# Feed-forward: three inner layers kept with the features on the partitions, and their sum of squares as one plain product with ones

## The reference

```python
amp = jax.nn.sigmoid(x @ amp_w + amp_b)
ph = jnp.tanh(x @ ph_w + ph_b) * math.pi
h = (jnp.cos(ph) + jnp.sin(ph)) * amp
for l in range(L):                                  # L = 2
    e = h @ ent_w[l] + ent_b[l]
    ent = e @ ent_pw[l] + ent_pb[l]
    h = _layer_norm(h + ent, ln3_g[l], ln3_b[l])
    t = jnp.einsum('bsd,pdf->pbsf', h, path_w[l]) + path_b[l][:, None, None, :]
    mod = jnp.cos(phase[l]) + jnp.sin(phase[l])
    interf = jnp.sum(t * mod[:, None, None, :], axis=0)
    h = _layer_norm(h + interf, ln4_g[l], ln4_b[l])
x = _layernorm(x + h)
```

## Time and profile before

| | |
|---|---|
| median of 3 runs | 908.15 us (905.5 to 908.82) |
| the profiled execution | 906.72 us, its span 904.8 us |
| mean granted TensorE clock | 0.989 |
| PE (matmul) | 861.6 us, 95% of the span |
| PE weight load | 717.6 us, 79% |
| DVE (VectorE) | 677.2 us, 75% |
| ACT (ScalarE) | 548.4 us, 61% |
| POOL (GpSimd) | 487.0 us, 54% |
| share of PE in the chain that ended last | 59% |

### The profile page before, as it was taken

One profiled execution on the slowest core, in us unless ns is written; L12 is line 12 of the kernel. 1 busy time (PEld: TensorE's weight loads), 2 busy tenths in 40 slices (PEclk: granted clock), 3 DMA queues, 4 the chain that ended last, 5 costly groups with the idle time before them and its releaser, 6 DMA issues.

```text
span 904.8 us, 19451 instructions
## 1 busy us (share of the span) xinstructions
PE 861.6 (95%) x5812; PEld 717.6 (79%) x5812; DVE 677.2 (75%) x2060; ACT 548.4 (61%) x1666; POOL 487.0 (54%) x796
## 2 busy tenths in 40 slices
PE   6899999999899999999999999998999999999993
PEld 6778888888787888888888887776778778878773
DVE  5778888888878878777787866758884675666556
ACT  6756556666666757575656655755736645664563
POOL 3465655465856646454655521337751781593387
PEclk9999999999999999999999999999999999999997
DMA  6655353543584846575584548434002002001001
GB/s 204 228 167 174 118 166 124 174 162 129 179 265 141 255 129 211 158 233 153 160 236 137 179 125 272 169 109 148 1 24 71 0 12 82 1 1 47 1 0 47
DMA packets 79475, 117.49 MB, mean 130 GB/s; under 512 B 8480, under 2 KB 42272, under 8 KB 78752
## 3 DMA queue, kind: packets, MB, share of 16 engines
q1 hardware_dynamic: 75792, 112.81, 40.1%
q10 hardware_dynamic: 3600, 3.68, 1.3%
HBM read 58.25 MB, written 17.31 MB: 84 GB/s over the span
## 4 chain that ended last, share of the span: by engine, by line
PE 59%; DVE 6%; POOL 2%; SPq 2%; issue 2%; ACT 2%; DMA 1%; POOLq 0%; DVEq 0%; ACTq 0%
PE bank L161 45%; PE bank L1513 4%; PE bank L2040 3%; PE bank L1536 2%; PE bank L1499 2%; PE bank L1540 1%; SPq L702 1%; DVE stats L1942 1%; DVE w_ffn L1727 1%; ACT prob L1106 1%; POOL hT L1835 1%; DMA xres<-in_x 1%; PE bank L1449 1%; DVE y L1956 1%; DVE bank L1257 0%
## 5 line engine op out<-in xcount | busy, mean ns | idle before, releaser
L1106 ACT ACTIVATE prob<-bank,nmax 128x128 f32<-128x128 f32 (+1 forms) x512 | 209.6, 432 | 25.8 <-DVE nmax L1257 23.3
L161 PE MATMUL bank<-w_ffn,hT 128*128 128x512 f32 x768 | 188.5, 396 | 1.1 <-DVE w_ffn L1727 0.9
L1257 DVE CUSTOM_DVE_ANT_0 bank<-bank,mask 128x128 f32<-128x128 f32 (+1 forms) x512 | 168.2, 386 | 3.4 <-DVE cv L1202 2.3
L161 PEld LDWEIGHTS bank<-w_ffn,hT 128*128 128x128 f32 x768 | 140.2, 188 | 29.9 <-POOL hT L1835 1.4
L919 POOL TENSOR_TENSOR zone<-raw,zone 128x256 fp32r<-128x256 f32 x128 | 96.3, 785 | 59.8 <-ACT zone L1053 59.8
L1513 PE MATMUL bank<-ident,prob 128*128 128x128 f32 x768 | 119.4, 278 | 0.8 <-ACT probT L1119 0.4
L1119 ACT ACTIVATE probT<-bank 128x512 f32<-128x512 f32 x97 | 58.5, 604 | 96.3 <-PE bank L1540 96.1
L1106 ACT ACTIVATION_READ_ACCUMULATOR prob<-bank,nmax 128x1 f32 x512 | 110.9, 217 | 0.0
L161 PE MATMUL bank<-xT,w_q 128*128 128x256 f32 x768 | 102.5, 286 | 3.0 <-DVE o L1278 3.0
L161 PEld LDWEIGHTS bank<-xT,w_q 128*128 128x128 f32 x768 | 98.9, 193 | 8.0 <-issue 3.1
L1896 ACT ACTIVATE ht<-bank,cols 128x128 f32<-128x128 f32 x192 | 72.4, 459 | 53.2 <-PE bank L2040 53.2
(11 more groups left out here) (133 smaller groups left out, 1510.4 us busy)
## 6 DMA issues: line engine op xcount, KB each, us to landing
q<-stage SPq DMA_DIRECT2D x192, 128.0 KB, 2.8
k<-kstage SPq DMA_DIRECT2D x48, 256.0 KB, 4.0
x<-xres SPq DMA_DIRECT2D x16, 512.0 KB, 4.6
raw<-in_ent_wT SPq DMA_DIRECT2D x32, 256.0 KB, 4.1
raw<-in_ent_pw SPq DMA_DIRECT2D x32, 256.0 KB, 4.4
raw<-in_path_w SPq DMA_DIRECT2D x8, 512.0 KB, 3.9
xres<-in_x SPq DMA_DIRECT2D x8, 512.0 KB, 4.0
x1b<-x SPq DMA_DIRECT2D x8, 512.0 KB, 5.1
```

The source lines that it names most:

```text
L161: ins = t.matmul(out, lhs(a, k), rhs(b, k), start=first and n == 0 and m == 0, stop=last and n == len(kts) - 1 and m == 2, skip_group_chec ...
L1106: ins = s.activation(prob[:, u, c * width:(c + 1) * width], banks[u][:, c * width:(c + 1) * width], ACT.Exp, scale=-1.0, bias=nmax[:, i % ...
L1257: ins = v.tensor_tensor_reduce(scored, scored, mask[:, S - width:S], scale=-1.0, scalar=3e38, op0=ALU.add, op1=ALU.min, accum_out=nmax[:, ...
```

## The change

**Layers 0 to 2** are made turned, so that nothing is transposed back: weights are stationary, hT moves, and the four banks `z0` to `z3` of a layer hold 128 features x 512 tokens each. The mean over the features is taken out beforehand: the matrix of each layer is centred over its output features and multiplied by the gain of the layer before (`means` on ScalarE, `centre` on VectorE), and its constants go into a column `c` (`column_sum`, `column_total`, `column_centred`, `bias_partials`), of which each inner layer has one. Left is the sum of squares: ScalarE squares the four banks, GpSimd and VectorE add them up, and TensorE multiplies by ones in a single plain fp32 product (`sum_of_squares`), which puts the sum over all features on every partition. ScalarE takes the inverse root, one Newton step refines it (`inverse_of`), and the factor is applied when the next layer's banks are read (`turned_out`).

**Layer 3** is as before with tokens on the partitions; its input's factor comes from four one-column products (`second_moments`) and a power on GpSimd.

```diff
+_SCALAR = ("hi0", "sq0", "sq1", "sq2", "sq3", "hi1", "hi2", "hi3", "root", "square")
+_VECTOR = ("z0", "z1", "z2", "z3", "lo0", "pair", "total", "lo1", "lo2", "lo3", "newton", "inverse")
...
+                def turned_out(s_, j):
...
+                    if s_ == 0:
+                        ins = v.tensor_copy(y[:, j, :], bank)
+                    else:
+                        ins = v.scalar_tensor_tensor(y[:, j, :], bank, -0.5 / D, inverse[:, :], ALU.mult, ALU.mult)
+                    ins.then_inc(s_zv, 1)
+                    v.wait_ge(s_zv, step_of(VECTOR_STEPS, b, s_, f"z{j}"))
+                    v.sem_inc(drained[plan.bank((f"z{s_}", j))], 1)
...
+                def sum_of_squares(s_):
+
+                    t.wait_ge(s_zv, step_of(VECTOR_STEPS, b, s_, "total"))
+                    k.wait_free(("s", s_))
+                    k.filled(("s", s_), t.matmul(banks[plan.bank(("s", s_))][:, :], ffn.ones[:, :], squares[0], start=True, stop=True))
...
+                for c in range(KT):
+                    turned_pass(0, c)
+                    if b == 0 and c == 0:
+                        column_sum(0)
+                    if b == 0 and c == 1:
+                        column_total(0)
...
+                for s_ in range(TURNED):
+                    wait_alone(g, s_za, step_of(SCALAR_STEPS, b, s_, "sq1"), s_passed)
+                    g.tensor_tensor(squares[0], squares[0], squares[1], ALU.add).then_inc(s_zp, 1)
+                    if s_ < TURNED - 1:
+                        for n in range(BT):
+                            residual(b, *divmod(BT * s_ + n, 2))
...
                     if t is last_cross and i == NG - 1:
                         s.preload_act_table_set("silu_and_others")
+                        ffn.means(s, 0)
                     if t is flush and i == 0:
                         s.wait_ge(s_kst, last_cross.lin(2 * LOADS, LOADS * (B + 2) - 2 * LOADS * B))
                         ffn.wait_columns(s)
                         gate(0)
+                        ffn.stage_hi(s, 0)
                         gate(1)
+                        ffn.means(s, 1)
                     if t is flush and i == 1:
                         gate(2)
-                        ffn.stage_hi(s, 0)
+                        ffn.stage_hi(s, 1)
+                        ffn.means(s, 2)
                         gate(3)
```

More of the change, by code:

```diff
@@ L340 @@
 GATES = ("ph", "amp")
-BY_VECTOR = ("eb",)
 UNITS_OF_STEP = 3
@@ L958, in body @@
                         split_ctx()
+                    if t is last_cross and i == NG - 1:
+                        ffn.residual_of_path(g, 1, ident)
+                    if t is flush and i == 0:
+                        ffn.bias_partials(g, 1)
             links = 0
@@ L2070, in tensor @@
+                if not last:
+                    for i in range(BT):
+                        k.wait_drained(("xt", i))
+                    for m in range(KT):
+                        gate(k, "ph", m)
+                        gate(k, "amp", m)
             every_block(t, body)
```

632 lines of the change are left out of this document (417 added, 215 removed).

## The result

The changed kernel takes 929.42 us (median of 4 runs, 929.12 to 931.84) against 907.8 for the kernel before in the same runs: ratio 1.0248, 95% interval 1.0221 to 1.0274. Slower by 22 us, as forecast in sign, and inside the range, 7 us above the forecast of 922.

The account below looks back on a forecast made before the run. TensorE was taken as the bound, VectorE at the end. Block 0 +14.3, blocks 1 and 2 -2.1, block 3 -1.6, last layer +3.3 sum to +13.9 us on the 908.15 median: 922, range 909 to 932.

Parts of the forecast that it names:

- The mechanism: Whole kernel: VectorE's queue decides in block 0 and partly at each layer change; 922 us, chance 0.67.
- 14.3: Block 0: gates start at 682.1 instead of 667.8, mainly from weight preparation in VectorE's and ScalarE's queues; +14.3 us.
- The copy at F: Flush, at the last probability transposes (F): ScalarE's four row means delay the copy TensorE waits for by 3.0 us.
- the gap's clock: Block 0, after the column-sum wait: clock at its lower level for some 3.3 us, half the work lost, 1.65 us.
- rival 3: Block 0: preparation is early enough, the column-sum wait and its clock loss vanish; +3 us, 911, chance 0.13.
- forecast -1.05: Blocks 1 and 2: removed transposes outweigh added products and waits; -1.05 us each, -2.1 together.
- "I take 1.3" for a change: Each layer change: TensorE waits for low halves, 0.6 to 1.6 us; 1.3 taken, nearer the rows with GpSimd contention.
- "0.45" for the second moments' wait: Last layer change of a block: high halves covered, second moments wait 0.45 us for the total of squares.
- "I take 1.2" for a group of one-column products: Second moments and similar groups: four one-column products, eight weight loads, 0.84 to 1.64 us; 1.2 taken.
- forecast +1.7: Block 3 to the end: -1.6 us up to the last layer, +3.3 for its later unit reads.
- Strict turns of VectorE and GpSimd: Layer changes: each engine waits out the other's instructions, 2.6 us a change; +24 us, 932, chance 0.12.
- TensorE alone deciding: Whole kernel: every wait hidden, only TensorE's own work counts; -9.2 us, 899, chance 0.08.

Follow-up runs that it names:

- the early column sum: Against the changed kernel, VectorE adds layer 0's column sums ahead of centring the third weight, TensorE's product over them stands behind three passes: 931.85 us, 1.0259.
- all edits: Changed kernel plus early column sum, late low halves, residual beside gates, VectorE's new order, earlier load, last amplitude first and later fourth high half: 915.09 us, 1.0099.
- the reordered kernels: Changed kernel with VectorE's first two low halves made earlier at layer changes: alone 925.26 us; with the other list moves and earlier load 915.13 and 915.09.
- the best orders: Changed kernel with list moves and earlier load together, 915.13 us (1.0086), and the same with block 0's last amplitude made first, 915.09 us (1.0099).
- the thirteen changed kernels: The changed kernel (929.42 us) and its twelve follow-up variants of order, load, doubled product, GpSimd's partial products and no centring: 915.09 to 938.73 us.

## Why the prediction was right, and where it was off

The time lies inside the range, but at its edge: 929.4 against the 929 of the forecast's own bounds. The mechanism came true: VectorE's queue decides in block 0 and in part at each change of layer. The size was kept together by errors that cancel and by 2.0 us of chance.

**Block 0.** By the clock of the execution all came as forecast: layer 0's first product at 613.68 (614.1), the column sum at 629.55 (630), the wait 9.44 (9.2), gates at 682.37 (682.1). This is partly luck, since this execution was 2.0 us early ahead of F. From there block 0 is 16.8 us longer and not 14.3. The copy at F came 2.4 us late (3.0), but behind TensorE's wait for it the granted clock was 0.50 in 586 to 588 and 0.71 in 588 to 590, and 24 products took 6.98 us instead of 5.85: the forecast had no term for that. Inside, errors cancelled. The centring under GpSimd's work takes 0.96 each and not the 0.55 of the forecast; the column sums come at 0.81 a group (616.48 to 617.29) instead of 1.2; the gap's clock cost about 1.3 (32 products in 9.12 against 7.84) instead of 1.65. That VectorE's queue makes the wait is shown by the early column sum and by leaving out the centring; what was wrong is the idea behind rival 3, that the wait's removal gives its length. It gave 1.9 us at most, since VectorE's remaining list is the next wait.

**Blocks 1 and 2**: forecast -1.05, measured +2.0 and +1.8. The steps that failed:
- "I take 1.3" for a change. It is 1.96, over the forecast's upper bound of 1.6. The model's times were near: at the change from layer 0 to 1 in block 1 (T = 718.5) the first low half was there at T + 2.9 (2.75), the total at T + 5.2 (5.05), the second low half at T + 6.4 (6.15). Its contended rows gave 1.6, and 1.3 was taken though the contention came in full; the rest is the short wait for a bank and the slower steps behind each wait. That the kernel with GpSimd's residual elsewhere has 1.30 is a coincidence, for the 1.3 was meant with it. At eight changes this is 5.3 of the 10.6 us by which the sum was short, of which the early start hid 2.0.
- The input's load was not in the sum at all: 0.84 and 0.36 us of waiting, 0.87 shorter in block 1 when it is issued earlier.
- "0.45" for the second moments' wait: the 24 products end by their pitch at 746.06 + 5.47 = 751.53, and the one-column products begin at 752.84, 1.3 later.
- "I take 1.2" for a group of one-column products: 0.81, under the forecast's lower bound of 0.84. This is the error that went the other way, 2.7 us over seven groups.
- The plain product was right: 0.86 forecast, 0.85 measured, and on the path.

Two slips stand in the working and weigh little. The gates of the kernel before start at 667.64, as 30 products at 0.228 give, and not at 667.8; and between the two waits of a change TensorE does 12 products, for which the 5.5 is right, and not 8.

**Block 3 and the end**: forecast +1.7, measured +4.0. Two changes give 1.3 of that, the chain of units the rest:

```profile
896.69 6.18 PE L2267 MATMUL bank<-w_ffn,hT 128*128 128x512 f32 x24
...
906.02 0.75 DVE L2132 SCALAR_TENSOR_TENSOR y<-bank,rstd,stage_bias 128x512 f32<-128x512 f32 x1 [1.30 <-POOL rstd L1974]
...
916.41 0.72 DVE L2132 SCALAR_TENSOR_TENSOR y<-bank,rstd,stage_bias 128x512 f32<-128x512 f32 x1
```

The first unit is read 9.3 us behind the last layer's start (8.5 forecast), the last 19.7 (18.3; 15.0 before).

**The rivals.** Strict turns of VectorE and GpSimd (2.6 a change) did not come: 1.96 with GpSimd's pieces beside, 1.30 without. The Trainium skill, "SBUF — State Buffer", section "SBUF: two separate sides", has whoever starts first block the other for the whole instruction. Here the two went side by side, each lengthened: in the 4.62 us of GpSimd's four pieces (720.83 to 725.45; 0.90 each in the kernel that has them beside the gates, so 3.6 alone) VectorE made the pair, the total and the second low half (0.68, 0.69 and 0.75 alone), 5.7 us of work without the parts of two more. TensorE alone deciding was far off as the change stood; with all edits blocks 1 and 2 come within 2.8 us of it.

So the time went to three places: block 0's preparation (2.4 us more of waiting at F, 9.4 at the column, and the low clock behind both), eight changes of 1.96 (15.7 us, order and contention, of which the reordered kernels keep some 2.5 at the changes from layer 0 to 1 of blocks 1 and 2), and the waits for input and moments; against them stands TensorE's smaller work. Of the 22 us the best orders return 13 to 15. The rest is in block 0, where VectorE's list of centring, splits and sums is longer than what TensorE has to do. No version that I ran beats the kernel before; a path bias folded without VectorE was not tried.

## What to carry to other kernels

A stage that needs all of the stage before is only as good as the order in which the vector engines empty the banks: make the first operand of the next stage before the last bank is read, and put sums and statistics behind the operands. Mind that the next stage also needs the banks: reading them later made TensorE wait there. Price a wait by what stands next in the releasing engine's list, not by its length. Work made once ahead of a loop is not hidden where the loop's own vector work starts at the same time; moved to GpSimd, it slowed what VectorE did beside it by as much as it took off. And before comparing stretches of two executions, look for a common point ahead of the first change: what runs before it can differ by more than the effect.

## What was not expected of the hardware

- **Clock dips without a long gap.** The 24 products behind the second moments, behind a wait of 0.60 us, took 5.69 to 5.76 us in 27 of the 39 blocks 1 to 3 of the thirteen changed kernels and 7.30 to 7.36 in the other 12 (block 1 five times, block 2 four times, block 3 three times), with a granted clock of 0.72 in 752 to 758 in one of them:

```profile
752.00:758.00 6.00, 5.61 (x22) 4.63 (x23) 3.34 (x7) 0.00 (x0) 1.98 (x3) 0.72 0.01 3
```

  Such a dip costs about 1.6 us, as much as one of these edits gives, and hit different blocks in different executions; what sets it off was not found. In block 0, where the 16 transposes of the input stand between the second moments and these products, none of the thirteen has one (5.80 to 5.84). At the head of layer 0, behind waits of 1.5 to 2.6 us, 12 products took 2.97 to 3.00 us in eight kernels; behind waits of 1.95, 2.56 and 3.04 they took 4.59, 4.38 and 4.58 in three others. So the length of the wait alone does not decide.
- **VectorE beside GpSimd.** An operation of VectorE with one large input (the centring, 0.55 alone) was slowed by GpSimd about as much as those with two: to 0.96. A bank read beside it stayed at 0.69.
- **One-column products** are cheap: a group of four passes in 0.81 us, 0.20 each (eight records).
